# Mixture-of-experts rows: stored once and gathered by lists of token numbers, with Wo^T, expert biases and the first slots' rows loaded earlier

## The reference

```python
x = x + attention(layernorm(x), Wq, bq, Wk, bk, Wv, bv, Wo, bo)      # 2048 x 512
xf = layernorm(x)
gate_logits = xf @ gate_w.T                                          # 2048 x 8
top_vals, top_idx = top_k(gate_logits, 2)
w = softmax(top_vals)
y_all = einsum("td,eod->teo", xf, expert_w) + expert_b
x = x + sum(take(y_all, top_idx) * w)
```

## Time and profile before

| | us |
|---|---|
| median of 3 runs | 1701.26 (1698.3 to 1703.56) |
| profiled execution, its own time | 1700.52 |
| its span in the trace | 1698.7 |
| TensorE busy | 1631.1 (96%) |
| VectorE, ScalarE, GpSimd busy | 1444.1, 1267.5, 567.0 |
| chain that ended last: PE, ACT, DMA, issue, DVE | 89%, 2%, 2%, 2%, 2% |
| read from HBM, written to HBM | 91.14 MB, 86.23 MB |

### The profile page before, as it was taken

One profiled execution on the slowest core, in us unless ns is written; L12 is line 12 of the kernel. 1 busy time (PEld: TensorE's weight loads), 2 busy tenths in 40 slices (PEclk: granted clock), 3 DMA queues, 4 the chain that ended last, 5 costly groups with the idle time before them and its releaser, 6 DMA issues.

```text
span 1698.7 us, 38136 instructions
## 1 busy us (share of the span) xinstructions
PE 1631.1 (96%) x13715; PEld 793.5 (47%) x13716; DVE 1444.1 (85%) x1749; ACT 1267.5 (75%) x2383; POOL 567.0 (33%) x827
## 2 busy tenths in 40 slices
PE   6999999999999999999999999999999999977995
PEld 3633444444444444444444444444444444656784
DVE  5388999999999999999999999999999973566565
ACT  3126888888888888888888888888888887304563
POOL 3121233333333333333333333333333345453222
PEclk9999999999999999999999999999999999988998
DMA  7345344423232334332323222322233014585476
GB/s 219 98 108 120 53 107 117 95 71 82 78 86 68 96 75 90 71 93 70 84 68 92 68 68 68 95 68 68 68 95 71 18 43 150 183 298 178 154 261 223
DMA packets 87863, 179.03 MB, mean 105 GB/s; under 512 B 21247, under 2 KB 25343, under 8 KB 86961
## 3 DMA queue, kind: packets, MB, share of 16 engines
q1 hardware_dynamic: 50464, 87.22, 21.8%
q0 software_dynamic: 34624, 88.25, 16.6%
q10 hardware_dynamic: 2640, 1.59, 0.4%
HBM read 91.14 MB, written 86.23 MB: 104 GB/s over the span
## 4 chain that ended last, share of the span: by engine, by line
PE 89%; ACT 2%; DMA 2%; issue 2%; DVE 2%; another core or an unknown queue 1%; SPq 0%; POOL 0%; ACTq 0%; DVEq 0%; POOLq 0%
PE bank L1071 35%; PE bank L1032 25%; PE bank L1061 16%; PE bank L1240 6%; PE bank L983 5%; ACT o_acc L869 1%; PE bank L1023 1%; PE bank L1269 1%; PE bank L1283 1%; DMA xs<-slots_x 1%; DMA at_lo<-at_parts 0%; DMA y_rows<-ys,tok_i 0%; PE bank L1042 0%; DMA k_parts<-parts 0%
## 5 line engine op out<-in xcount | busy, mean ns | idle before, releaser
L1381 DVE TENSOR_REDUCE max_kc<-bank 128x1 f32<-128x1024 f32 x1024 | 1243.2, 1222 | 65.3 <-PE bank L1032 48.6
L892 ACT ACTIVATE arena_p<-bank 128x512 f32<-128x512 f32 x2048 | 1109.7, 595 | 173.4 <-PE bank L1061 137.0
L1071 PE MATMUL bank<-arena_p,v_cur 128*32 128x256 f32 x8192 | 655.2, 392 | 10.6 <-ACT o_acc L869 10.6
L1032 PE MATMUL bank<-k_st,q_st 48*128 48x512 f32 x2048 | 511.0, 496 | 0.8 <-ACT qf L839 0.8
L1061 PE MATMUL bank<-q_st,k_st 50*128 50x512 f32 x2048 | 441.3, 405 | 0.8 <-ACT arena_p L892 0.8
L1032 PEld LDWEIGHTS bank<-k_st,q_st 48*128 48x128 f32 x2048 | 190.5, 183 | 428.4 <-issue 398.7
L1061 PEld LDWEIGHTS bank<-q_st,k_st 50*128 50x128 f32 x2048 | 295.1, 185 | 31.8 <-ACT arena_p L892 17.2
L1071 PEld LDWEIGHTS bank<-arena_p,v_cur 128*32 128x32 f32 x8192 | 163.0, 108 | 297.5 <-issue 156.1
L534 POOL DMA_DIRECT2D sums<-o_acc x128 | 64.8, 513 | 342.8 <-ACT o_acc L869 337.9
L537 POOL DMA_DIRECT2D sums_rec<-sums x32 | 18.2, 570 | 212.0 <-DVE sums L1411 212.0
L983 PE MATMUL bank<-xT,arena_p 128*128 128x512 f32 x160 | 84.8, 644 | 2.1 <-ACT xT L830 2.1
(11 more groups left out here) (205 smaller groups left out, 1017.6 us busy)
## 6 DMA issues: line engine op xcount, KB each, us to landing
slots_x<-pad_row POOLq DMA_DIRECT2D x27, 1295.0 KB, 6.0
q_st<-q_parts SPq DMA_DIRECT2D x192, 128.0 KB, 4.6
xs<-slots_x SPq DMA_DIRECT2D x39, 259.0 KB
q_parts<-parts SPq DMA_DIRECT2D x16, 512.0 KB, 3.3
we_raw<-in_L_ffn_expert_w POOLq DMA_DIRECT2D x8, 1024.0 KB, 6.4
at_parts<-o_hl POOLq DMA_DIRECT2D x128, 64.0 KB
we_his<-o_hl POOLq DMA_DIRECT2D x32, 256.0 KB, 2.4
we_hi<-we_his SPq DMA_DIRECT2D x8, 1024.0 KB
```

Of the source, the lines that this page charges most:

```text
L892: act.activation(probs[:, u % PRING, :], bank[:, ring_bank(("score", u)), :], ACT.Exp, scale=SCALE).then_inc(p_ready, 1)
L1032: return pe.matmul(bank[:, 2 + 2 * (m % 2) + q, :], q_st[r:r + CROW, j % SLOTS, h, qt * P:(qt + 1) * P], k_st[r:r + CROW, key_slot(j // NC ...
L1071: mm = pe.matmul(bank[32 * h:32 * h + 32, 6, half], v_cur[:, kt, :], probs[:, (REP * kt + h) % PRING, half], start=(kt == 0 and part == 0) ...
L1381: dve.reduce_max(max_kc[:, m:m + 1], bank[:, 2 + 2 * (m % 2):4 + 2 * (m % 2), :].rearrange("p a s -> p (a s)"), AX.X).then_inc(m_done, 1)
```

## The change

- slots_x (17280 rows of 518 floats) goes. x_rows holds each token's row once, and 128 rows of padding; ids_x holds a 4-byte token number per slot row, filled once (fill_lists) with the numbers of padding rows.
- ScalarE issues the store of each tile's rows (store_row, 265 KB) after the next tile's root. POOL scatters token numbers instead of rows (place_ids, 512 bytes each, again two per tile): chunk 0 ahead of the last residual load, two tiles of chunk 1 in the last division, the rest of chunks 1 and 2 after it, chunk 3 beside slots 1 to 4.
- SP loads a slot's 128 numbers (load_ids, 512 bytes); POOL gathers the rows by them (gather_slots, an indirect DMA of 265 KB). The first four are issued before the slots.
- Wo^T comes as an input of its own by one DMA in round 28; turn_wo and its copies go. wo_gates is at steps 11 and 13, not 14 and 15.
- The biases' buffer is cleared before the output projection, loaded behind attention chunk 2, and split at tile 9.
- Experts 5 and 6 are loaded ahead of attention chunk 3. The last tile multiplies upper x lower second, and expert 7 is loaded from there on (hi_used).
- ranks(3) stands behind slot 0's products and place_rows(3) and the lists behind it one slot later. `chosen`, `before` and the ones of the shifted terms are bf16.
- The fourth add_bias_o moves from behind the last division into it. The buffers of slots and of the final sums lie in other places.

```diff
     BROWS = BLO + E
 
-    slots_x = nc.dram_tensor("slots_x", [NX * P, W], F32).ap()
+
+    x_rows = nc.dram_tensor("x_rows", [T + P, W], F32).ap()
...
 
 
-        TURN_WO, WO_GATES = (11, 12), (14, 15)
-        LOGITS_AT, BACK_AT, RANKS_AT = {3: 2, 12: 3}, {4: 2, 13: 3}, {7: 2, 15: 3}
...
+            no_ids = slot_i[:, :, :].rearrange("p a n -> p (a n)")[:, 0:FILL]
+            pool.iota(tok_u[:, :], [[P, NKT]], base=0, channel_multiplier=1).then_inc(ids_step, 1)
+            pool.iota(no_ids, [[0, FILL]], base=T, channel_multiplier=1).then_inc(ids_step, 1)
+            pool.wait_ge(ids_step, 2)
+
+            def place_ids(n):
+
                 c = n // TT
                 if n == 0:
-                    pool.wait_ge(fill_dma, 16 * -(-NX // FILL))
-                    pool.wait_ge(tok_ready, NC - 1)
+                    pool.wait_ge(fill_dma, 16 * FILLS)
                 if n % TT == 0:
                     pool.wait_ge(slots_ready, c + 1)
-                    if c == NC - 1:
-                        pool.wait_ge(tok_ready, NC)
-                pool.wait_ge(nmr_ready, n + 1)
                 for a in range(2):
-                    pool.indirect_dma_start(slots_x, bass.IndirectOffsetOnAxis(ap=slot_i[:, a, n:n + 1], axis=0),
-                                            x2_all[:, n, :], None).then_inc(sc_dma[c], 16)
+                    pool.indirect_dma_start(ids_x, bass.IndirectOffsetOnAxis(ap=slot_i[:, a, n:n + 1], axis=0),
+                                            tok_u[:, n:n + 1], None).then_inc(id_dma[c], 16)
+
+            def gather_slots(s):
+
+                b = s % SR
+                pool.wait_ge(ids_dma[b], 16 * (s // SR + 1))
+                if s == 0:
+                    for c in range(EARLY_C):
+                        pool.wait_ge(row_dma[c], 16 * TT)
+                    pool.wait_ge(be_ready, 1)
+                if s == 2:
+                    pool.wait_ge(gl_full, NC)
+                if s == S1:
+                    for c in range(EARLY_C, NC):
+                        pool.wait_ge(row_dma[c], 16 * TT)
+                if s >= SR:
+                    pool.wait_ge(xt_full, s - SR + 1)
+                    pool.wait_ge(meta_read, s - SR + 1)
+
+                of = x_rows[0:EARLY_C * CH, :] if s < S1 else x_rows
+                pool.indirect_dma_start(xs[b][:, :], None, of,
+                                        bass.IndirectOffsetOnAxis(ap=ids[:, b:b + 1], axis=0)).then_inc(xs_dma[b], 16)
 
             def divide_outputs(i):
 
@@ -536,12 +576,13 @@
                 pool.wait_ge(rec_ready, i)
                 pool.dma_start(sums_rec.rearrange("h (a q) -> (h a) q", a=32), sums[:, :]).then_inc(rec_dma, 16)
                 if i == N:
-                    scatter(0)
+                    add_bias_o(NC - 1)
                 pool.wait_ge(rec_dma, 16 * i)
                 for h in range(REP):
                     pool.dma_start(rec_b[32 * h:32 * h + DK, :], sums_rec[h].partition_broadcast(DK)).then_inc(recb_dma, 16)
                 if i == N:
-                    scatter(1)
+                    place_ids(TT)
+                    place_ids(TT + 1)
                 pool.wait_ge(recb_dma, 16 * REP * i)
                 pool.tensor_tensor(o_acc[:, :], o_acc[:, :], rec_b[:, :], ALU.mult).then_inc(o_norm, 1)
...
+            def fill_lists():
+                pool.dma_start(x_rows[T:T + P, :], pad_row[:, :]).then_inc(fill_dma, 16)
+                for z in range(0, NX, FILL):
+                    pool.dma_start(ids_x[z * P:(z + FILL) * P, :].rearrange("(p n) o -> p (n o)", p=P), no_ids
+                                   ).then_inc(fill_dma, 16)
...
                 divide_outputs(i)
-                if FILL * (i - 1) < NX:
-                    fill_rows(FILL * (i - 1))
+                if i == 1:
+                    fill_lists()
...
+            for n in range(TT):
+                place_ids(n)
             residual(NC - 1)
             divide_outputs(N)
-            for n in range(2, TT):
-                scatter(n)
-            add_bias_o(NC - 1)
 
...
-            for n in range(TT, (NC - 1) * TT):
-                scatter(n)
-            for t in range(TT):
-                place_outputs(t)
-                scatter((NC - 1) * TT + t)
-            for s in range(TT, NS):
+            for n in range(TT + 2, (NC - 1) * TT):
+                place_ids(n)
+            for s in range(SR):
+                gather_slots(s)
+            for s in range(NS):
+                if s + SR < NS:
+                    gather_slots(s + SR)
                 place_outputs(s)
+                if 1 <= s <= TT:
+                    place_ids((NC - 1) * TT + s - 1)
...
+                if i == N - SLOTS:
+                    sp.dma_start(wo_t[:, :, :], Wo_t.rearrange("(j p) k -> p j k", p=P)).then_inc(wt_dma, 16)
...
-            def load_slots(s):
-                b = ring(s)
-                if not first_pass(s):
-                    wait_first(xt_full, number(s) - SR + 1)
-                    wait_first(meta_read, number(s) - SR + 1)
-                row = sp.value_load(row_i[0:1, bass.ds(number(s), 1)], min_val=0, max_val=(NX - 1) * P)
-                sp.dma_start(xs[:, b, :], slots_x[bass.ds(row, P), :]).then_inc(xs_dma[b], 16)
+            def load_ids(s):
+                b = s % SR
+                if s >= SR:
+                    sp.wait_ge(xs_dma[b], 16 * (s // SR))
+                row = sp.value_load(row_i[0:1, s:s + 1], min_val=0, max_val=(NX - 1) * P)
+                sp.dma_start(ids[:, b:b + 1], ids_x[bass.ds(row, P), :], allow_slow_non_contiguous=True).then_inc(ids_dma[b], 16)
...
             sp.wait_ge(eh_dma, 16 * E * KD)
             sp.wait_ge(pv_done, PRING // REP + NKT * N)
             load_attention(2)
+            sp.wait_ge(be_zero, 1)
+            for r in (0, BLO):
+                sp.dma_start(be_raw[r:r + E, :], expert_b).then_inc(be_dma, 16)
             sp.wait_ge(sums_dma, 16 * REP * N)
             load_hi(0)
             sp.wait_ge(recb_dma, 16 * REP * N)
             for e in (1, 2):
                 load_hi(e)
             sp.wait_ge(wo_full, TT)
-            load_hi(5)
+            for e in (5, 6):
+                load_hi(e)
             load_attention(3)
-            load_hi(6)
-            sp.wait_ge(be_zero, 1)
-            for r in (0, BLO):
-                sp.dma_start(be_raw[r:r + E, :], expert_b).then_inc(be_dma, 16)
+            for c in range(EARLY_C):
+                sp.wait_ge(id_dma[c], 32 * TT)
+            sp.wait_ge(list_ready, 1)
+            for s in range(SR):
+                load_ids(s)
             sp.wait_ge(wo_full, TT * 3)
             for e in (3, 4):
                 load_hi(e)
-            sp.wait_ge(wo_full, NKT)
+            sp.wait_ge(hi_used, 1)
             load_hi(7)
-            for c in range(EARLY_C):
-                sp.wait_ge(sc_dma[c], 32 * TT)
-            sp.wait_ge(list_ready, 1)
-            for s in range(S1):
-                load_slots(s)
+            for s in range(SR, S1):
+                load_ids(s)
             for c in range(EARLY_C, NC):
-                sp.wait_ge(sc_dma[c], 32 * TT)
+                sp.wait_ge(id_dma[c], 32 * TT)
             sp.wait_ge(list_ready, 2)
             FIRST_BACK = S_EARLY + 4
             for s in range(S1, NS):
                 if s == S2:
                     sp.wait_ge(list_ready, 3)
-                load_slots(s)
+                load_ids(s)
                 n = s - FIRST_BACK
...
+            def store_row(n):
+                c = n // TT
+                if n % TT == 0:
+                    act.wait_ge(sum_ready, c + 1)
+                    act.wait_ge(tok_ready, c + 1)
+                act.wait_ge(nmr_ready, n + 1)
+                act.dma_start(x_rows[n * P:(n + 1) * P, :], x2_all[:, n, :]).then_inc(row_dma[c], 16)
+
             for n in range(NKT):
                 if n in LOGITS_AT:
                     logits_evac(LOGITS_AT[n])
                 deviation2(n)
+                if 1 <= n <= (NC - 1) * TT:
+                    store_row(n - 1)
+            for n in range((NC - 1) * TT, NKT):
+                store_row(n)
 
             def transposed_hi(s):
...
@@ -1103,19 +1159,11 @@
                     projection_step(p, k)
             pe.wait_ge(proj_evac, LAST)
 
-            def turn_wo(j):
-
-                if j == 0:
-                    pe.wait_ge(wo_dma, 16)
+            def wo_gates(part):
+
+                if part == 0:
+                    pe.wait_ge(wt_dma, 16)
                     pe.wait_ge(m_done, 2 + MUNITS * N)
-                for k in range(KD):
-                    mm = pe.transpose(bank[:, 2 + j, k * P:(k + 1) * P], wo_raw[:, k, j * P:(j + 1) * P], ident[:, :])
-                mm.then_inc(woT_full, 1)
-
-            def wo_gates(part):
-
-                if part == 0:
-                    pe.wait_ge(woT_evac, KD)
                     for j in range(KD):
                         mm = pe.matmul(bank[32 * j:32 * j + 32, LG_BANK, :], wg_sb[:, j, :], wo_t[:, j, :],
```

(25 more changed lines are left out.)

105 lines of the change are left out of this document (60 added, 45 removed).

## The result

The changed kernel takes **1794.03 us** (median of 4 runs, 1790.25 to 1798.73); beside it the kernel before took 1699.78 (1697.52 to 1703.56). The ratio is 1.055, interval 1.0528 to 1.0573: slower by 94 us. Forecast were 1695, with a range to 1707.

What follows compares the result with a forecast made beforehand. TensorE's work alone was taken to bound the attention, with gains only in its gaps between 1461 and 1540. Terms -2.0 -1.4 +4.1 +0.3 -14.6 +1.0 +2.1 +4.0 = -6.5 us gave 1694.0, stated as 1695; range 1684 to 1707.

Steps and rivals of the forecast that it cites:

- part 2: POOL's new order around the last residual load: eight placings ahead of it delay chunk 2's attention load, +4.1 us.
- part 3: Stretch from tile 12 to slot 0: 18.3 us instead of 32.9 with lighter scatters, -14.6 us.
- the meeting with the residual: Residual's 1 MB meets the 2 MB attention load issued at 1462: bounds 0 and 2.6 us, 2.6 taken.
- Turned Wo, -2.0: Output projection's 16 Wo transposes on TensorE go: -2.0 us, round 30 shorter by 2 us.
- bf16 ranks, -1.4: Rank products in bf16 instead of float32: 0.45 us saved on each of three ahead of the slots, -1.4.
- The fourth attention load has more than 10 us in hand: Last attention load, some 4 us later, is not used until about 1507, so it costs nothing.
- The stall: Between tile 12 and slot 0, TensorE busy 3.83 of 9 us; goes with the heavy scatters, likelier than not.
- Part 4, +6.1: Slots: list then gather replace one direct load; +2.1 us up to slot 9, +4.0 at slots 27 and 35.
- the ranks' +1.0: Chunk 3's ranks now follow slot 0's products: +1.0 us.
- C: Rival: in the slots, gathers on POOL become the pace, every slot late, 1710 us; chance 0.12.
- A: Rival: the stall before slot 0 stays, made by any full DMA stretch, 1706 us; chance 0.20 including nothing moving.
- the four: Rivals: stall stays, or waits only change names (0.20 together); losses cushioned, 1684 (0.18); gathers pace the slots (0.12).

Runs made afterwards that it cites:

- pairs: GpSimd waits until each tile's previous two scatters have landed: kernel before 1.0106; changed kernel with numbers 512 bytes apart, placings behind the division, lists early 1.0116.
- group 3: Runs beside the kernel before at 1689.9 us; added bursts of eight scatters left attention rounds at 40.9 to 41.0 us.
- group 1: Runs beside the kernel before at 1699.7 us; added bursts of eight scatters made attention rounds 51.4 to 54.2 us, undisturbed 40.9.
- all three kernels with numbers apart: Changed kernel with numbers as rows of 512 bytes (1.009), as 4 bytes 512 bytes apart (1.0084), or as rows of 64 bytes (1.007).
- the one 512 apart: Changed kernel writing the same 4-byte numbers to addresses 512 bytes apart: 1715.8 us, 1.0084 of before.
- the kernel with the lists early: Changed kernel with numbers 512 bytes apart and eight list buffers instead of four, lists loaded four slots earlier: 1.0068 of before.
- the one with the placings behind: Changed kernel with numbers 512 bytes apart, placings ahead of the residual moved behind the last division: 1.0098 of before.
- groups 1 and 4: Runs beside the kernel before at 1699.7 and 1702.3 us; added bursts of eight scatters made attention rounds 49.7 to 54.2 us, undisturbed 40.9.
- the probes: Changed kernel with bursts of eight added scatters in some attention rounds: 1859.77, 1790.26, 1784.29, 1835.25 and 1849.85 us, one execution each.
- groups 3 and 5: Two groups of runs on the same chip; the kernel before took 1689.9 us in one and 1701.5 in the other.
- fours: Kernel before with turned Wo from memory and bf16 ranks, GpSimd waiting after every four row scatters until they landed: 1692.90 us, 0.9945.

## Why the prediction was wrong

**The step that failed** is in part 2: "one placing costs 0.96 to 1.00 plus 0.30 whatever it carries, I assume". That is the price on GpSimd, and it was right. I put none on the transfer itself; in part 3 I even counted it as relief ("those bursts are 512-byte ones"). Measured by the run that changes nothing but the addresses, the 32 scatters of adjacent numbers cost 78 us: while 4096 writes of 4 bytes went out, two loads of the attention output came so late that TensorE waited 20.75 and 55.67 us. I had no row for it; the bounds I set (0 and 2.6 us for the meeting with the residual) were taken from large transfers, and none of the rivals had the scatters' own transfer as its mechanism. The Trainium skill ("DMA: Bandwidth & Descriptors", Anatomy of one DMA) would have given 2.0 us for a placing by its formula. Here adjacent numbers took 33.5 us, and numbers 512 bytes apart, in pairs that wait, 2.2 to 6.3 with a median of 3.1; so it is near for the second kind and far off for the first.

With that cured, the other terms can be checked on the kernel with numbers 512 bytes apart (span 1716.2, so +17.5, where I had said -6.5):

- **Turned Wo, -2.0**: right (0.9988; round 30 41.5 us where it was 43.6 by the starts of GpSimd's sums, and 40.4 in the changed kernel). **bf16 ranks, -1.4**: no effect seen at the end.
- **Part 2, +4.1**: the mechanism is there, in group 3, where nothing holds the engines. With the placings ahead, chunk 2's attention load took 10.6 us beside the residual's and TensorE waited 2.68; with the placings behind, 8.7 and 0.77. Forecast was a wait of about 3. In group 1 a second cost lies over it. Round 31 took 46.1 to 46.3 us in all three kernels with numbers apart (42.7 before), since the burst stands in it and in that group holds the engines: TensorE sat 2.17 and 0.99 us at its end in the one 512 apart. The load took 10.0 us there as well, but TensorE came later and waited 0 to 1.78. "The fourth attention load has more than 10 us in hand" was too much. Beside the adjacent numbers it cost 55.67 us, and even with the placings 512 bytes apart behind the division TensorE waited 2.40 for it. From the kernel with the lists early, and then the one with the placings behind:

```profile
1468.96 1.39 PE L1197 MATMUL bank<-at_hi,wowc 128*32 128x512 f32 x8 [2.68 <-DMA at_lo<-at_parts]
```

```profile
1467.62 1.06 PE L1191 MATMUL bank<-at_hi,wowc 128*32 128x512 f32 x8 [0.77 <-DMA at_lo<-at_parts]
```

- **Part 3, -14.6**: from chunk 3's logits to slot 0's product 34.8 us before, 26.5 now: 8.3 of it came (from tile 12 on, 24.6 us where I had 18.3). VectorE is last, as said (slot 0's transposes wait 8.78 us for the chain behind it). The stall was named as made by the scatters and not by full DMA engines: that inference is borne out in groups 1 and 4, where the probes make it out of scatters alone. But I concluded that small scatters would not make one, and there they do.
- **Part 4, +6.1**, with the ranks' +1.0: slots took 162.9 us against 139.5, +23.4. Places were right (slot 9, and slots 27 and 35 behind SyncE's waits), sizes not: the two waits cost 10.5 together and not 4.0, since the list's load and the gather are one after the other and the gather then queues behind a placing of outputs; and the gaps up to slot 9 cost 9.1 in group 1 (47.9 against 38.8) and not 2.1. In group 3, where nothing held the engines, they took 42.0 and 43.1, where the kernel before with turned Wo took 35.9 in the same group: 6 to 7. The rest of the 23.4, some 4 us, lies in the last thirty slots too.
- **Rivals**: C asked for a slower pace of all slots and did not happen (3.4 us apart). A, that the stall stays, is not what took the rest: at its place TensorE sat idle 0.5 us in this kernel. What came was none of the four.

Before slot 0: forecast -13.6, measured -5.7. Behind it: forecast +7.1, measured +23.4. Adjacent numbers: forecast 0, measured +78. The sum of the first two alone would have been 1716 us and outside my range too, so the late lists and GpSimd's row beside the first slots are a second failed step, in part 4, by themselves enough to miss.

What stays open: why adjacent writes slow the packets of other queues, and why so much more beside large loads; why bursts of indirect DMAs hold all engines in some groups of runs and not in others, also on one and the same chip (groups 3 and 5); whether the taking of the records has a part in it; and how long a burst may be where it happens.

## What to carry to other kernels

When a scatter of rows is replaced by one of indices, give every index a stretch of memory of its own (rows of 64 bytes were enough, 4 bytes were not): the issuing engine's trace does not show the price, the packets of all other queues do. Ask of every new transfer what it does to the queues beside it, not only what its instruction costs, and if no row shows it, put the bound up to the waits it could cause. Breaking rows of indirect DMAs by a wait for their landing can pay where there is slack (fours: 0.9945; pairs cost 1% in both kernels tried). Measure on more than one occasion, since the same kernel differed by 66 us between two, and compare a profile only with profiles of the same kind.

## What the runs showed of the hardware that I had not expected

- DMA engines that count as busy (0.77) at 6 GB/s: 22 packets took 8.4 us each behind a burst of adjacent 4-byte writes. With 4-byte writes 512 bytes apart, or rows of 64 bytes, the kernel loses none of those 78 us. Where no such load stood beside it, a burst of eight had landed after 8.9 us (512 bytes apart: 5.3) and cost no more than the other forms.
- Eight indirect DMAs back to back from GpSimd stop VectorE, ScalarE and then TensorE for 3 to 5 us and are followed by 6 to 38 us at half clock: 9 to 20 us a burst, whether 4 or 512 bytes an element; eight plain DMAs do not. This was so in two groups of runs (before: 1700 and 1702 us) and not in two others (1689 and 1690), and the kernel before, which scatters its rows in such a burst, differs by as much as one hold between them; that this is the whole difference is an inference.
- The same bursts are where the trace has lost records of landings (28 of 128 kept, against 128 of 128 where nothing was held). A profile whose rows of DMA issues lack their time to landing may be one in which the engines were held.
